# A four-layer cross-attention chain on one core: output weights split during the last batch, flags between residuals, and narrow products in two banks

## What is computed

```python
# layer 0: one-head attention over ctx, a sigmoid gate, RMS norm
# layers 1 and 3 (the gated layers)
q, k, v = heads(layernorm(x) @ Wq * 0.125), heads(ctx @ Wk), heads(ctx @ Wv)   # 16 heads of 64
out = softmax(mask(q @ k.T)) @ v
x = x + tanh(attn_gate) * (out @ Wo)              # Wo: 1024 x 256
h = gelu(layernorm(x) @ W1) @ W2                  # W1: 256 x 1024, W2: 1024 x 256
x = x + tanh(ff_gate) * h
# layer 2 (counted from 0; the "third layer")
vm = type[t] == 1 and type[t + 1] == 1            # flags: which of two expert weights a token takes
x = x + where(vm, self_attn(rms(x)) @ v_dense, ... @ l_dense)   # rotary, causal
ck, cv = split(ctx @ ckv_w)                       # the narrow products, 16 heads of 8
x = x + (softmax((rms(x) @ cq_w) @ ck.T) @ cv) @ cdense_w
x = x + where(vm, mlp_v(rms(x)), mlp_l(rms(x)))
```

## Time and profile before

| what | us |
|---|---|
| median of 3 runs | 2456.26 (2452.11 to 2456.43) |
| the profiled execution | 2455.51 |
| its span, first to last instruction | 2453.5 |
| TensorE busy in the span | 2332.8 (95%) |
| VectorE busy | 1580.9 (64%) |
| ScalarE busy | 1280.9 (52%) |
| POOL busy | 618.6 (25%) |

### The profile page before, as it was taken

One profiled execution on the slowest core, in us unless ns is written; L12 is line 12 of the kernel. 1 busy time (PEld: TensorE's weight loads), 2 busy tenths in 40 slices (PEclk: granted clock), 3 DMA queues, 4 the chain that ended last, 5 costly groups with the idle time before them and its releaser, 6 DMA issues.

```text
span 2453.5 us, 41140 instructions
## 1 busy us (share of the span) xinstructions
PE 2332.8 (95%) x16032; PEld 1894.9 (77%) x16032; DVE 1580.9 (64%) x4256; ACT 1280.9 (52%) x2186; POOL 618.6 (25%) x680
## 2 busy tenths in 40 slices
PE   7978999999999999789999999799999999999999
PEld 4857999999999785356666666446799999999978
DVE  3257777777777557666676676313777777777764
ACT  2135555555555433267777777311555555555543
POOL 0024344443443205100000000001344344344320
PEclk8789999999999999899999999999999999999999
DMA  8720112111110110000000000300011112111010
GB/s 268 194 76 20 45 42 57 33 54 45 42 45 26 53 37 18 26 26 26 27 26 26 26 14 2 123 25 10 20 45 42 45 42 57 37 50 45 26 52 16
DMA packets 36099, 115.96 MB, mean 47 GB/s; under 512 B 4586, under 2 KB 18514, under 8 KB 35906
## 3 DMA queue, kind: packets, MB, share of 16 engines
q1 hardware_dynamic: 33442, 101.04, 13.6%
q10 hardware_dynamic: 2464, 12.29, 2.0%
HBM read 112.40 MB, written 0.92 MB: 46 GB/s over the span
## 4 chain that ended last, share of the span: by engine, by line
PE 85%; DVE 10%; ACT 3%; DMA 1%; issue 1%; ACTq 0%; SPq 0%; DVEq 0%
PE bank L999 19%; PE bank L986 18%; PE bank L1011 12%; PE bank L535 7%; DVE n_scores L1856 5%; PE bank L1737 4%; PE bank L1724 4%; PE bank L1749 3%; PE bank L1961 3%; PE bank L631 2%; PE bank L1973 2%; PE bank L1710 2%; PE bank L829 1%; PE bank L1021 1%; PE bank L619 1%; PE bank L1706 1%
## 5 line engine op out<-in xcount | busy, mean ns | idle before, releaser
L1060 ACT CAST p_T_high<-bank 125x512 fp32r<-125x512 f32 x672 | 350.6, 595 | 517.3 <-PE bank L1011 517.3
L1133 DVE TENSOR_TENSOR p_T_low<-bank,p_T_high 125x512 fp32r<-125x512 f32 x672 | 422.5, 684 | 256.8 <-ACT p_T_high L1060 256.7
L1099 DVE CUSTOM_DVE_ANT_0 scores<-bank,mask 128x500 f32<-128x500 f32 x672 | 418.2, 672 | 1.4 <-PE bank L986 1.4
L1070 ACT ACTIVATE scores<-scores,row_max 128x1500 f32<-128x1500 f32 x224 | 353.4, 1578 | 9.1 <-DVE row_max L1104 9.1
L999 PE MATMUL bank<-p_T_high,keys_nat_high 125*128 125x256 f32 (+1 forms) x1152 | 346.0, 300 | 1.7 <-ACT inverse L1067 1.7
L999 PE MATMUL bank<-p_T_high,keys_nat_low 125*128 125x256 f32 (+1 forms) x1152 | 346.3, 301 | 0.0
L999 PE MATMUL bank<-p_T_low,keys_nat_high 125*128 125x256 f32 (+1 forms) x1152 | 346.2, 300 | 0.0
L1011 PE MATMUL bank<-ident,scores 128*125 128x128 f32 x2688 | 331.0, 273 | 2.3 <-ACT scores L1070 2.3
L1011 PEld LDWEIGHTS bank<-ident,scores 128*125 128x125 f32 x2688 | 318.5, 187 | 5.0 <-ACT scores L1070 4.8
L1856 DVE CUSTOM_DVE_ANT_0 n_scores<-bank,n_zeros 112x500 f32<-112x500 f32 x384 | 237.4, 674 | 131.2 <-PE bank L1724 131.2
L986 PE MATMUL bank<-keys_T_high,q_stage_high 128*128 128x500 f32 x672 | 282.3, 420 | 9.8 <-DVE q_stage_low L1076 6.9
(11 more groups left out here) (223 smaller groups left out, 3473.3 us busy)
## 6 DMA issues: line engine op xcount, KB each, us to landing
ctx_T<-in_ctxT SPq DMA_DIRECT2D x32, 750.0 KB, 4.3
ctx_nat<-in_ctx SPq DMA_DIRECT2D x32, 672.0 KB
q_and_o<-in_ctxT SPq DMA_DIRECT2D x16, 750.0 KB, 10.2
n_ctx_T<-in_ctxT SPq DMA_DIRECT2D x16, 750.0 KB, 4.1
q_and_o<-in_ctx ACTq DMA_DIRECT2D x16, 672.0 KB
mask_bytes<-in_mask SPq DMA_DIRECT2D x32, 187.5 KB, 5.2
weights<-in_L_W SPq DMA_DIRECT2D x4, 1024.0 KB, 10.0
ctx_nat<-in_ctx SPq DMA_DIRECT2D x32, 78.0 KB
```

The lines of the kernel that those rows point to most:

```text
L1060: e.copy(PTs[0][g % 2][0:KP, 4 * c:4 * c + 4, lo:lo + 128], psum[3 + c][0:KP, :].rearrange("p (k r) -> p k r", k=4)).then_inc(s_eh, 1)
L1070: e.activation(SB[s % 2], SB[s % 2], ACT.Exp, bias=mx[:, s % 4, 3:4], accum_out=mx[:, s % 4, 4:5]).then_inc(s_ex, 1)
L1099: e.tensor_tensor_reduce(out=SB[u % 2][:, c * CHK:(c + 1) * CHK], in0=psum[c][:, 0:CHK], in1=mb[:, c * CHK:(c + 1) * CHK], scale=1.0, scal ...
L1133: e.tensor_tensor(low, psum[3 + c][0:KP, :].rearrange("p (k r) -> p k r", k=4), high.bitcast(F32), ALU.subtract).then_inc(s_el, 1)
```

## The change

**Wo.** The load of Wo leaves `sp_gated_b` and becomes `sp_wo`, two DMAs behind the last keys of the attention, which wait until the batch before the last has made its scores and sums. They go where that batch's keys lay, and to 512 columns beyond. POOL splits it in three parts behind its last work of the attention, ahead of the join, with six instructions; ScalarE's and VectorE's instructions for it are gone. TensorE waits for POOL's parts. Both gated layers are changed alike.

**Flags.** `dve_flags` loses its last instruction (now `dve_rope`, at the old place) and moves to behind `dve_rows` of the first four tiles.

**Narrow products.** They alternate between banks 7 and 6, so that product i waits until product i - 2 is out. Bank 6 is shared with the sums: the first sum of a batch also waits for the last product's way out, product 1 for the output of an earlier batch, and `output` moves to the front of its slot.

```diff
@@ build: buffers
+        wo_high_5 = sbuf("wo_high_5", D, F32R, scope=rounded)
+        rounded.close()
         mask_raw = sbuf("mask_bytes", KEYS, U8)
...
         kt_raw = [sbuf(f"ctx_T{i}", KEYS, scope=loaded) for i in range(2)]
         kn_raw = [sbuf(f"ctx_nat{i}", KT * C, scope=loaded) for i in range(2)]
+        loaded.close()
+
+        wo_high_a = sbuf("wo_high_a", 5 * D, F32R, scope=loaded)
+        sbuf("to_ctx_nat0", 2 * 1504 - 5 * D, scope=loaded)
+        wo_a = sbuf("wo_a", 6 * D, scope=loaded)
+        sbuf("over_ctx_nat1", KT * C, scope=loaded)
+        wo_b = sbuf("wo_b", 2 * D, scope=loaded)
+        wo_high_b = sbuf("wo_high_b", 2 * D, F32R, scope=loaded)
+        loaded.close()
+        sbuf("to_wo_a", 2 * 1504, scope=loaded)
+        wo_low_a = sbuf("wo_low_a", 6 * D, F32R, scope=loaded)
+        sbuf("to_wo_b", KT * C, scope=loaded)
+        wo_low_b = sbuf("wo_low_b", 2 * D, F32R, scope=loaded)
         loaded.close()
...
-        wo_r = chunks(W_r, 0, 8, D), chunks(W_r, 4096, 8, D)
...
+        wo_parts = [(wo_high_a, wo_low_a[:, 0:5 * D], wo_a[:, 0:5 * D]),
+                    (wo_high_5, wo_low_a[:, 5 * D:6 * D], wo_a[:, 5 * D:6 * D]), (wo_high_b, wo_low_b, wo_b)]
+        wo_r = by_chunk(wo_high_a, wo_high_5, wo_high_b), by_chunk(wo_low_a, wo_low_b)
@@ sp_gated_b, and a new function on SP's queue, called behind sp_cross of each gated layer
-            e.dma_start(g_wo, io[f"L{l}_Wo"].rearrange("(k p) n -> p k n", p=128)).then_inc(s_w[f"l{l}o"], 16)
...
+        def sp_wo(e, on, x, l):
+
+            on.wait_ge(*x.scores((B - 1) * RT - 1, 2))
+            on.wait_ge(*x.sums((B - 1) * NG - 1))
+            wo = io[f"L{l}_Wo"].rearrange("(k p) n -> p k n", p=128)
+            e.dma_start(wo_a.rearrange("p (k n) -> p k n", k=6), wo[:, 0:6, :]).then_inc(s_w[f"l{l}o"], 16)
+            e.dma_start(wo_b.rearrange("p (k n) -> p k n", k=2), wo[:, 6:8, :]).then_inc(s_w[f"l{l}o"], 16)
@@ pool_cross, at its end
+            on.wait_ge(*x.scores((B - 1) * RT - 1, 2))
+            on.wait_ge(s_w[f"l{gated.l}o"], 32)
+            for steps, part in zip(gated.wo_cut, wo_parts):
+                cut(e, on, steps, *part)
@@ pe_gated
-            on.wait_ge(*g.wo_cut)
+            for steps in g.wo_cut:
+                on.wait_ge(*steps[1])
@@ act_gated
-                if (j, half) == (4, 1):
-                    on.wait_ge(s_w[f"l{g.l}o"], 16)
-                    e.copy(wo_r[0], g_wo).then_inc(s_wo_high, 1)
@@ dve_gated
-                if (j, half) == (5, 1):
-                    on.wait_ge(*g.wo_high)
-                    e.tensor_tensor(wo_r[1], g_wo, wo_r[0].bitcast(F32), ALU.subtract).then_inc(s_cut, 1)
...
             dve_rows(e, on, g.ff_norm, 0)
+            if g.rope is not None:
+                dve_flags(e, on)
             dve_residual(e, on, g.wo, g.l - 1, g.ff_norm, TILES[1][:-1])
...
             if g.rope is not None:
-                dve_flags(e, on, g.rope)
+                dve_rope(e, on, g.rope)
@@ n_prod_bank
-            return psum[i] if b == 0 else psum[7]
+
+            return psum[i] if b == 0 else psum[7 - i % 2]
@@ pe_narrow, product(b, i)
-                if b >= 1:
-                    on.wait_ge(*(n_prod_out(b, i - 1) if i else n_prod_out(b - 1, 5)))
-                    on.wait_ge(s_n_rrc, b - 2)
+                if b >= 1 and i >= 2:
+                    on.wait_ge(*n_prod_out(b, i - 2))
+                elif b >= 2:
+                    on.wait_ge(*n_prod_out(b - 1, 4 + i))
+                    if i == 0:
+                        on.wait_ge(s_n_rrc, b - 2)
+                    else:
+                        on.wait_ge(s_n_own, b - 2)
@@ pe_narrow, sums(b, lo) and recip_T(b)
-                if b and lo == 0:
+                if lo == 0:
+                    on.wait_ge(*n_prod_out(min(b + 2, B - 1), 5))
                     on.wait_ge(s_n_own, b)
...
-                on.wait_ge(*n_prod_out(min(b + 2, B - 1), 5))
+                on.wait_ge(*n_prod_out(min(b + 2, B - 1), 4))
@@ dve_narrow, the loop over slots
+                if s >= 13 and (s - 13) % 6 == 0:
+                    output((s - 13) // 6)
                 if s < SLOTS:
                     maxima(s)
...
-                if s >= 13 and (s - 13) % 6 == 0:
-                    output((s - 13) // 6)
             output(B - 1)
```

More of the change, by code:

```diff
@@ L387, in plan @@
                 self.ao_high = {x: ao_high_steps.step() for x in self.value}
-                self.wo_high, self.wo_cut = wo_high_steps.step(), cut_steps.step()
+                self.wo_cut = [high_low(w_cut_steps) for _ in wo_parts]
                 self.w1_cut = [high_low(w_cut_steps) for _ in range(2)]
@@ L1134, in dve_cross, with pool_cross, halve @@
                                         high.bitcast(F32), ALU.subtract).then_inc(s_el, 1)
-        def pool_cross(e, on, x):
-            def cut(high, low, src, sem, value, moving=False):
+        def pool_cross(e, on, x, gated):
+            def halve(high, low, src, sem, value, moving=False):
                 if moving:
@@ L1149, in keysT @@
                     on.wait_ge(*x.scores((b - 1) * RT - 1, 2))
-                cut(KTs[0][b % 2][:, cols], KTs[1][b % 2][:, cols], kt_raw[b % 2][:, cols],
+                halve(KTs[0][b % 2][:, cols], KTs[1][b % 2][:, cols], kt_raw[b % 2][:, cols],
                     *x.keysT(b, c))
@@ L1157, in keys @@
                     on.wait_ge(*x.sums((b - 1) * NG - 1))
-                cut(KNs[0][b % 2][0:KP, cols], KNs[1][b % 2][0:KP, cols], kn_raw[b % 2][0:KP, cols],
+                halve(KNs[0][b % 2][0:KP, cols], KNs[1][b % 2][0:KP, cols], kn_raw[b % 2][0:KP, cols],
                     *x.keys(b, c))
@@ L1308, in pool_gated @@
             on.wait_ge(*prod.made[g.value[7, 1]])
-            cut(e, on, g.w2_cut, w2_r[0], w2_r[1], g_w2)
+            cut(e, on, g.w2_cut, QO_r[:, 0:2048], W_r[:, 8192:10240], g_w2)
             if g.rope is not None:
@@ L1350, in dve_flags, with dve_rope @@
                             tidx[0:S, 0:1], None, ALU.is_equal).then_inc(s_rope, 1)
+        def dve_rope(e, on, i):
             on.wait_ge(*prod.made[i])
@@ L1699, in product @@
             def product(b, i):
-                bank7 = n_prod_bank(b, i)
+                at_bank = n_prod_bank(b, i)
                 on.wait_ge(s_n_ctx[b % 2], 16 * (b // 2 + 1))
-                if b >= 1:
-                    on.wait_ge(*(n_prod_out(b, i - 1) if i else n_prod_out(b - 1, 5)))
-                    on.wait_ge(s_n_rrc, b - 2)
+                if b >= 1 and i >= 2:
[6 more added lines that the diff above has]
+                        on.wait_ge(s_n_own, b - 2)
                 if i < 3:
-                    m = e.matmul(bank7[:, 0:CHK], wck, KT2[b % 2][:, i * CHK:(i + 1) * CHK], start=True, stop=True)
+                    m = e.matmul(at_bank[:, 0:CHK], wck, KT2[b % 2][:, i * CHK:(i + 1) * CHK], start=True, stop=True)
                 else:
@@ L1709, in product @@
                         at = (4 * (i - 3) + k) * KP
-                        m = e.matmul(bank7[0:KP, C * k:C * k + C], KT2[b % 2][:, at:at + KP], wcv,
+                        m = e.matmul(at_bank[0:KP, C * k:C * k + C], KT2[b % 2][:, at:at + KP], wcv,
                                      start=True, stop=True)
@@ L2023, in sync @@
             sp_cross(e, on, layers[0], False)
+            sp_wo(e, on, layers[0], 1)
             on.wait_ge(s_join, ENGINES * J["l1"])
@@ L2033, in sync @@
             sp_cross(e, on, layers[1], False)
+            sp_wo(e, on, layers[1], 3)
             on.wait_ge(s_join, ENGINES * J["l3"])
@@ L2109, in gpsimd @@
             join(e, on, J["l1q"])
-            pool_cross(e, on, layers[0])
+            pool_cross(e, on, layers[0], g1)
             join(e, on, J["l1"])
@@ L2117, in gpsimd @@
             join(e, on, J["l3q"])
-            pool_cross(e, on, layers[1])
+            pool_cross(e, on, layers[1], g3)
             join(e, on, J["l3"])
```

26 lines of the change are left out of this document (14 added, 12 removed).

## The result

The changed kernel took 2417.6 us, the median of 4 runs (2411.0 to 2425.8), against 2456.35 before: a ratio of 0.9847 with a 95% interval of 0.9814 to 0.9880. The forecast was 2411, its range 2403 to 2430. Five more runs of the same kernel gave 2422.3 (ratio 0.9853, 0.9836 to 0.9871); the median of all nine is 2418.9. So the gain is about 37 us where 45 were forecast. The profiled execution is the fastest of the nine, 2411.01 us with a span of 2409.2, and the forecast for it, 2410.6, was met by terms that were wrong in both directions. That is what the rest is about.

A forecast was written before the change was run, and what follows sets the result against it. TensorE, with 85% of the chain, was taken as the bound, time being won only at its stops and the slow clock behind them. 4.63 + 5.06 + 4.1 + 23.1 + 8.0 = 44.9 us less gave 2411 us, range 2403 to 2430.

The forecast's parts named there:

- Wo, layer 1: Before layer 1's first Wo matmul: the 2.96 us idle and 1.67 us of slow clock go, 4.63 us together.
- flags: Before the rotary matmuls: 3.18 us idle and 1.14 of slow clock go, less 0.2 residual delay; 4.1 us.
- Wo, layer 3: Before layer 3's first Wo matmul: the 3.39 us idle and 1.67 us of slow clock go, 5.06 us together.
- The cover of Wo: POOL's six split instructions for layer 1's Wo end at about 815, 17 us before the join, so cost nothing.
- Narrow products, steady state: Fourteen narrow-attention batches: the second bank removes product waits, 23.2 + 3.7 - 3.8 for ScalarE's limit = 23.1 us.
- The bound by weight loads: Narrow attention: weight loads' waits of 23.2 us plus 3.7 for broken matmul overlap give an upper bound of 27.
- the one by matmuls: Narrow attention's lower bound: counting only the array's idle share, 7.9 of 10.4, turns 23.2 us into 17.6.
- Narrow start: First narrow batches, without fills: 5.27 us idle before three products and 2.7 of slow clock go; 8.0, bounds 5 and 10.
- rival B: Slow clock at rotary matmuls, Wo and narrow start belongs to the kind of work; 7.2 us stay, 2418.6; chance 0.12.
- A: Narrow attention: ScalarE paces the product slots, so 14 us of the gain are lost, 2425 us; chance 0.17.
- C: Narrow attention: sums sharing bank 6 wait for ScalarE's late copy of the sixth product; 55 us lost, 2466; chance 0.03.
- D: Narrow attention: VectorE's maxima hold the slots anyway, the second bank changes nothing; only 13.8 us go, 2442.5; chance 0.03.

The follow-up runs named there:

- experiment 6: Changed kernel with each batch's sixth product taken out by VectorE instead of ScalarE, from the second batch on: 2415.6 us, ratio 0.9836 to the kernel before.
- experiment 7: Changed kernel with 6 and 12 transposes, results unused, filling the two stops left at the narrow start: 2418.4 us, ratio 0.9843 to the kernel before.

## Why the prediction came out as it did

**Right in direction and mechanism.** All stops that the change was said to remove are gone, and each cover held; in the stages that the change touches the only new stop is 0.28 us a batch. What was wrong are sizes, above all those of the slow clock. The time is 0.3% above the forecast and inside the range; the gain is 37 of 45 us.

**Wo, layer 1, and flags** (4.63 + 4.1 = 8.7): with both, the stretch from the last value product to the narrow scores was 185.0 to 188.1 us in the ten traces that have both, against 194.4 and 196.1 in the two that have neither: 6.3 to 11.1 us less. Right as a sum. But taken one by one the terms hold only for the trace that they were read from. The cost of a stop is its idle time, which repeats within 0.4 us (2.79, 2.96 and 3.15 before Wo, 3.18 three times before the rotary matmuls), and the slow clock behind it, which does not: 0.3, 1.7 or 3.0 us for the stop before Wo, 1.5, 3.1 or 4.2 for the other. Two of the traces have one stop removed; the third (the banks alone) has both, so it isn't the removal alone that changes a share. The flags alone measured 7.7 us, not 4.1.

**Wo, layer 3** (5.06): 4.3 us in the traces, 83.3 to 79.0. The idle 3.39 is gone and the first six tiles took 17.28 as said; the matmuls behind them took 34.7 instead of 34.5 and what follows the last of them 5.2 instead of 4.5.

**The cover of Wo**: the forecast had the split ending near 815, 17 us ahead of the join. It ended at 808.8 in a trace in which everything there is 5.9 us earlier (826.07 for the first value product, 831.97 before): 814.7, and 17 us.

**Narrow products, steady state** (23.1): 1.50 us for each batch in the even part, 20 to 21 us in all. The step that failed is the one that took back half of the sixth products' wait, 3.8 us, for ScalarE. The right place and the right engine, but the cost is 0.36 to 0.41 a batch, 5.0 to 5.7 us (experiment 6). 27, the upper bound, less 5.7 is 21.3, which is close to what came. The bound by weight loads was the right one, and not the one by matmuls, whose idle time in the same table is 15.9 us in all (7.9 + 3.2 + 3.0 + 1.8), less than the 17.6 that the prediction scaled it to.

**Narrow start** (8.0): the term took the slow clock in three places to be due to the three waits. Those waits are gone in every trace, but two stops remain there (0.76 and 1.62 us, experiment 7), and behind them the clock falls in most traces: the first batch took 21.7, 23.3, 24.9, 24.9, 24.9, 27.8 and 27.8 us with two banks (and 24.5 with the sixth product moved) against 27.2, 30.4, 30.7 and 30.7 with one. On average that is 4.7 us and not 8.0 (29.7 and 25.0), below the prediction's lower bound of 5. The size is rival B's for this stage, 8.0 - 2.7 = 5.3. Its reason, the kind of work, is not shown: the same work ran at 1.00 in one trace, and the two stops that remain are a reason as good.

**The drain** was not in the prediction at all: + 4.9 us. It is the largest single miss. I read the stops of the stages that the change touches, and left out that a change of the stage before could change what a stop behind it costs.

**The sum**, with typical values: 8 + 4.3 + 20.5 + 4.7 - 4.9 = 32.6 us, against 33.6 and 38.7 us as the medians of the two sets show. The profiled execution of the changed kernel reached the forecast because a third thing went its way: near 100 us, in work that the change doesn't touch, it ran at a mean clock of 0.82 where the one before had 0.51 (first row the kernel before).

```profile
96.00:124.00 28.00, 26.75 (x115) 25.41 (x115) 3.27 (x8) 1.38 (x3) 0.00 (x0) 0.51 0.41 111
```

```profile
96.00:124.00 28.00, 26.03 (x143) 23.15 (x144) 4.54 (x11) 5.17 (x9) 4.51 (x4) 0.82 0.56 170
```

Whoever had compared these two traces alone would have found 44.3 us, and each of the forecast's big terms confirmed.

**The rivals.** A holds in small, 5 us of its 14. B holds in size at the narrow start alone; in the drain a slow clock came where there was none, and it went when the stops were filled, which is not B. C did not come: the first sums wait for nothing. D did not come: the slots got shorter, and the maxima still wait for scores, 88.3 us in 74 waits between 1050 and 1520 us.

The Trainium skill, "TensorE: Matmul & The Clock Gate", Part 1, has the throttled state as the default, from which activity releases the engine. The windows agree as far as they go: filled with transposes whose results nobody uses, the drain ran at 1.00 twice. They also show what this rule by itself does not settle, that one and the same stop of 1.72 us is followed by 0.60 or by 1.00.

## What to carry to other kernels

Price a stop of TensorE as two terms: its idle time, which repeated within 0.4 us here, and the slow clock behind it, for which one trace gives a single draw (0.3 to 4.2 us for stops of some 3 us in this study); put a range on the second from every stop of about the same length that the traces show, and count stops that remain, not only those that go. When a gain is made of such terms, take a second trace of an unchanged kernel before believing a stage by stage agreement. And when a bank gets a second user, the instruction that empties it has to move ahead in its engine's list: without that, 18 of 20 us were gone here.

## What the runs showed of the hardware that I had not expected

- The same stop of 1.72 us, ending 11.7 us behind the last scores, in the same order of work, was followed by a fall of the clock in all eight traces of kernels with two banks and by none in the four with one. Shifting it by 1.5 us left the fall as it was (drain 208.2 us), by 1.9 us shortened it (205.9), and the fall began anything from 0.2 to 2.3 us behind the stop. The cause is open.
- 19 transposes whose results are thrown away, in the idle time of the drain, shortened it by 4.2 us (207.7 to 203.5) in the trace. That such transposes steady the time is not shown: the runs with 37 of them spread over 3.8 us, and those of two kernels with none spread as little (3.6 in four runs with the sixth product moved, 3.4 in six with Wo and flags), while the changed kernel's nine spread over 15.
- A stop of 2.79 us before Wo was followed by the full clock (the banks alone), stops of 2.96 and 3.15 us in the same place by half of it.
- At the narrow start the same instructions took 21.7 to 27.8 us for one batch, with the granted clock of the stretch at 1.00 and at 0.81, while every steady batch took 30.07 us to within 0.01.
